# A four-layer graph network on one core: PSUM bank offsets from a table instead of register arithmetic on TensorE

## The chip, the core and the metric

The kernel runs on one core of one Trainium2 chip. The metric is the device time of one execution in microseconds (us); lower is better. Three executions of the kernel before took 2623.59, 2626.45 and 2630.86 us; the median is 2626.45 us.

## What is computed

There are 3125 nodes with 512 features and 53,125 edges (50,000 drawn, and a loop at each node), sorted by target node. Four layers follow one another; each normalizes the features, takes the positive part, applies its own graph operation and adds the result to x:

```
h = relu(layernorm(x));  x = x + relu(segment_sum((h @ W)[src] * w, dst))                     # layer 0
h = relu(layernorm(x));  x = x + relu(segment_sum(norm * (h @ W.T + b)[src], dst))            # layer 1
h = relu(layernorm(x));  x = x + mlp(h + segment_sum(h[src], dst))                            # layer 2
h = relu(layernorm(x));  x = x + gat(h, src, dst)     # layer 3: 8 heads, softmax over a node's edges
```

In every layer the heavy part is the same: for each edge a row of 512 numbers is fetched by its source node and summed into the row of its target node.

## The kernel before

Nodes are cut into 25 tiles of 125. The edges are cut into chunks of 128; since a chunk can touch two tiles, 440 **steps** cover all of them, and which tile a step belongs to depends on the data. In each layer all 440 steps run in order. Step i of a layer does this:

- **GpSimd (POOL)** issues one indirect DMA (L1758 in layers 0 to 2, L1813 in layer 3) that gathers the 128 source rows of the step, 128x512, from a table in HBM into one of 11 ring buffers. From the twelfth on it first waits on `stepped`, until the step eleven before is done with that buffer. In layer 3, 25 of the 440 gathers were made earlier (L1805).
- **VectorE (DVE)** makes `sel`, a 128x125 matrix that says which edge goes to which node (L776 in layer 0; L483 for four steps at a time in layers 1 to 3). In layer 3 it also scales the gathered rows (L1218).
- **TensorE (PE)** multiplies `sel` with the gathered rows into a PSUM bank and adds to what is there (L1456; L1452 and L1453 on two float16 halves in layer 2; in layer 3 a small second product of 8 columns, L1458). One f32 matmul of the program stands in the profile as two records.
- **ScalarE (ACT)** waits for the last step of a tile, takes the bank out (`keep_tiles`, L1266 to L1272), and sets the bank up for the tile three further on (`set_bank`), which counts up the semaphore `fresh`.

Three banks (`NAGG`) are used in turn. TensorE must know a step's bank and that it has been set up. Both depend on the step's tile number t, which is known only at run time. So TensorE's instruction queue loads the tile numbers of 20 steps into registers (`load_tiles`, L1427, every 20 steps), and for each step copies one (L1430), adds 25 for each earlier layer plus one (L1448), waits on `fresh` for that sum, and computes the sum modulo 3 and from it the address. This queue is the part of TensorE that reads instructions, waits on semaphores and works on registers (PEldq in the profile); the array behind it multiplies.

Between the steps TensorE does other work of the layer: projections of the next layer's rows (L1416), transposes (L1405), small products (L1495, L1597, L1615, L1626). Between layers 2 and 3 stands a stretch of attention scores, in which TensorE uses the tile numbers too (`target_steps`); the change leaves it as it is.

The tables of step numbers are made at the end of the start-up, beside the projection of layer 0's rows. `step_tables` is a generator on VectorE whose pieces run in the order of the code between the pieces of the projection: `rows_low` (L470), which makes the low half of a tile's rows `hTl` for the projection on TensorE (L1416). The last piece of `step_tables` starts at L608, takes the turned tables out of PSUM (L608 to L611), works out the ends of tiles (L612 to L620) and a mask (L623 to L628). After it stand the last two `rows_low`. Then TensorE projects the last two tiles, ScalarE copies them out, SyncE stores them to `table[0]`, and the first gather of layer 0 waits for that store.

## Time and profile before

| | |
|---|---|
| device time, median of three | 2626.45 us |
| span of the profiled execution, first to last instruction | 3086.3 us |
| mean granted TensorE clock in it, share of full | 0.896 |
| TensorE busy (array) | 2384.8 us, 77% |
| GpSimd busy | 1795.9 us, 58% |
| VectorE busy | 1593.7 us, 52% |
| ScalarE busy | 335.0 us, 11% |
| moved by DMA | 557.12 MB, mean 181 GB/s |

The profiled execution took 460 us longer than the median of the executions without a profile, so its durations can't be taken over one for one. Of one execution the page gives the span from the first to the last instruction and nothing around it.

A group of instructions has a line of the code, an engine, the tile that is written and those that are read, a count, the busy time and the mean of one. "idle before" is the time that the engine stood still just before, and "<-" names what ended it; "issue" means that nothing in the profile explains it. For a gather on POOL the time shown is that of issuing it, not of moving its data.

### The profile page before, as it was taken

The page shows a single profiled execution, that of the slowest core. Times are in us where ns is not written, and L with a number is a line of the kernel's source. Part 1 is how long each engine was busy: PE and PEld are TensorE (multiplying, and loading weights), DVE is VectorE, ACT ScalarE, POOL GpSimd, SP SyncE. Part 2 cuts the span into 40 slices and gives each one's busy share as a digit, 9 for nine tenths or more (in the row PEclk, how much of TensorE's full clock was granted, in tenths as well). Part 3 has the DMA queues.
Part 4 walks back from the last instruction along what each step waited for, and adds up shares of the span by engine and source line. Part 5 has one row for each costly group of instructions (what it writes and reads, how often), then busy time and mean ns, then how long its engine had stood idle before and what let it go on. Part 6 is the DMA issues. An engine that isn't in the chain of part 4 may idle for free.

```text
span 3086.3 us, 32808 instructions
## 1 busy us (share of the span) xinstructions
PE 2384.8 (77%) x8542; PEld 1265.4 (41%) x8542; DVE 1593.7 (52%) x3774; ACT 335.0 (11%) x523; POOL 1795.9 (58%) x1878
## 2 busy tenths in 40 slices
PE   7888889887678777785788888885068589988887
PEld 5534444343223222221354454453058445544444
DVE  7665555554234353332244444444059677766665
ACT  4200000000000000000000000001057310000000
POOL 0466666665466666665666666653710456666665
PEclk9898999998789888997899999997579789999999
DMA  6586666676567766666666666663134457776665
GB/s 157 174 243 180 174 180 177 187 241 177 154 192 212 203 201 205 196 193 181 184 200 198 204 200 199 204 181 80 10 101 153 136 157 211 208 222 192 194 190 171
DMA packets 212761, 557.12 MB, mean 181 GB/s; under 512 B 55433, under 2 KB 56834, under 8 KB 212601
## 3 DMA queue, kind: packets, MB, share of 16 engines
q0 software_dynamic: 144448, 462.60, 52.3%
q1 hardware_dynamic: 66970, 90.10, 9.7%
q10 hardware_dynamic: 1182, 2.33, 0.3%
q8 instruction: 96, 1.57, 0.2%
q14 instruction: 65, 0.52, 0.1%
HBM read 515.28 MB, written 39.59 MB: 180 GB/s over the span
## 4 chain that ended last, share of the span: by engine, by line
PE 51%; DVE 15%; another core or an unknown queue 13%; issue 12%; DMA 6%; POOL 2%; ACT 1%; SPq 0%; ACTq 0%; DVEq 0%; POOLq 0%
PE tiles L1456 28%; DMA ring<-table,src_t 5%; PE upper L1416 5%; PE last_bank L1597 2%; PE tiles L1453 2%; PE tiles L1452 2%; DVE sel L776 2%; PE upper L1458 2%; PE last_bank L1416 2%; PE upper L1687 1%; POOL ring L1758 1%; PE upper L1626 1%; PE upper L1405 1%; DVE stage L713 1%
## 5 line engine op out<-in xcount | busy, mean ns | idle before, releaser
L1758 POOL DMA_INDIRECT ring<-table,src_t x1320 | 1266.9, 960 | 717.8 <-issue 324.3
L1456 PE MATMUL tiles<-ring,sel 128*125 128x512 f32 x2590 | 1390.4, 652 | 264.2 <-issue 178.4
L1456 PEld LDWEIGHTS tiles<-ring,sel 128*125 128x125 f32 x2590 | 444.3, 198 | 754.6 <-issue 745.5
L1813 POOL DMA_INDIRECT ring<-table,src_t x415 | 399.0, 961 | 240.5 <-PE upper L1458 105.5
L483 DVE TENSOR_TENSOR sel<-iota_bank,dl_t 128x500 f32<-128x500 f32 (+1 forms) x330 | 221.5, 674 | 513.3 <-PE tiles L1456 226.6
L1218 DVE TENSOR_TENSOR ring<-ring,last_bank 128x512 f32<-128x512 f32 x388 | 260.5, 685 | 169.6 <-DMA ring<-table,src_t 140.6
L1458 PEld LDWEIGHTS upper<-big,sel 128*125 128x125 f32 x880 | 169.7, 193 | 222.5 <-issue 222.0
L1452 PE MATMUL tiles<-ring,sel 128*125 128x512 f16 x440 | 176.5, 401 | 61.8 <-issue 32.1
L1453 PE MATMUL tiles<-ring,sel 128*125 128x512 f16 x440 | 172.9, 393 | 10.6 <-issue 10.3
L1416 PE MATMUL upper<-wh,hTh 128*125 128x512 f32 x200 | 100.4, 502 | 73.1 <-DVE hTl L759 23.7
L1791 POOL DMA_INDIRECT big<-score_table,src_t x104 | 98.4, 946 | 81.5 <-DVE acc L988 50.1
L776 DVE TENSOR_SCALAR sel<-node_iota,dl_t,w_t 128x125 f32<-128x125 f32 x440 | 134.2, 358 | 0.3 <-PE tiles L1456 0.2
L1458 PE MATMUL upper<-big,sel 128*125 128x8 f32 x880 | 126.2, 215 | 0.6 <-issue 0.6
L713 DVE TENSOR_TENSOR stage<-iota_bank,stage 128x500 bf16<-128x500 f32 x110 | 74.3, 676 | 86.5 <-remote 60.4
L1805 POOL DMA_INDIRECT x<-table,src_t x25 | 26.3, 1052 | 155.5 <-DMA acc<-src_digits 144.6
L1452 PEld LDWEIGHTS tiles<-ring,sel 128*125 128x125 f16 x440 | 61.2, 139 | 130.0 <-issue 111.8
L1597 PE MATMUL last_bank<-big,stage 128*125 128x512 f32 x200 | 96.8, 629 | 8.9 <-issue 7.3
L1093 DVE TENSOR_REDUCE big<-upper 128x16 f32<-128x448 f32 x84 | 50.6, 618 | 83.7 <-remote 72.4
L1405 PE MATMUL upper<-ident,stage 125*128 125x125 f32 x400 | 61.6, 277 | 41.2 <-ACT stage L1231 20.6
L1416 PE MATMUL upper<-wl,hTh 128*125 128x512 f32 x200 | 93.3, 466 | 0.0
L1416 PE MATMUL upper<-wh,hTl 128*125 128x512 f32 x200 | 92.1, 461 | 0.0
L1416 PEld LDWEIGHTS upper<-wh,hTh 128*125 128x125 f32 x200 | 45.9, 230 | 98.2 <-issue 85.0
(335 smaller groups left out, 2522.2 us busy)
## 6 DMA issues: line engine op xcount, KB each, us to landing
ring<-table,src_t POOLq DMA_INDIRECT x1735
table<-stage SPq DMA_DIRECT2D x50, 224.0 KB
table<-acc SPq DMA_DIRECT2D x50, 224.0 KB
acc<-dst_places SPq DMA_DIRECT2D x28, 256.0 KB
x<-dst_places SPq DMA_DIRECT2D x27, 256.0 KB
x<-in_x SPq DMA_DIRECT2D x25, 224.0 KB
kept_x<-x SPq DMA_DIRECT2D x25, 224.0 KB
x<-kept_x SPq DMA_DIRECT2D x25, 224.0 KB
```

Source lines behind the costliest of these rows:

```text
L483: V.tensor_tensor(to, iota_p[:, None, :].to_broadcast([CE, SB, TN]), dl_t[:, i:i + SB, None].to_broadcast([CE, SB, TN]), ALU.is_equal).the ...
L713: V.tensor_tensor(lo_hot[:, i % (2 * SB):i % (2 * SB) + SB, 0:TN], iota_p[:, None, :].to_broadcast([CE, SB, TN]), s_lo[:, i:i + SB, None]. ...
L776: V.tensor_scalar(out=sel[:, i % SELS, :], in0=node_iota[:, :], scalar1=dl_t[:, i:i + 1], scalar2=w_t[:, i:i + 1], op0=ALU.is_equal, op1=A ...
L1218: V.tensor_tensor(slot, slot, weights[:, :, None].to_broadcast([CE, H, DP]), ALU.mult).then_inc(scaled, 1)
L1416: last = P.matmul(to, a[:, q, k, :], b[:, k, :], start=(k == 0 and n == 0), stop=(k == KB - 1 and n == 2))
L1452: P.matmul(to, sel16[:, n % SELS, :], ring16[:, r, 0:D], start=False, stop=True, skip_group_check=True)
L1453: last = P.matmul(to, sel16[:, n % SELS, :], ring16[:, r, D:2 * D], start=False, stop=True, skip_group_check=True)
L1456: last = P.matmul(to, sel[:, n % SELS, :], rows, start=False, stop=True, skip_group_check=True)
L1458: last = P.matmul(upper[0:TN, bass.ds(b, 1), DEN_AT:DEN_AT + H].rearrange("p a h -> p (a h)"), sel[:, n % SELS, :], exps[:, i, :], start=F ...
L1597: last = P.matmul(bank[7][0:TN, :], yT[:, b, :], raw_w[:, b, :], start=(b == 0), stop=(b == KB - 1))
L1758: G.indirect_dma_start(out=(ring16 if layer == 2 else ring)[:, n % RING, :], out_offset=None, in_=table[layer][:, :], in_offset=bass.Indir ...
L1813: G.indirect_dma_start(out=rows_at(i), out_offset=None, in_=table[3][:, :], in_offset=bass.IndirectOffsetOnAxis(ap=src_t[:, i:i + 1], axis ...
```

## The change

The step's bank and the number to wait for are put into a table, `step_row`, once, at the end of the start-up. It has 22 groups, one for each 20 steps; a group holds 20 bank offsets (t modulo 3, times 512) and 10 numbers t + 1, one for each pair of steps, taken from the pair's second step. VectorE makes it with five more instructions after L611 of before, in the last piece of `step_tables`; the count of `tables` goes from 6 to 8.

TensorE loads 30 registers every 20 steps in place of 20. It takes the bank's offset straight from a register, and it waits on `fresh` only at even steps, for the bank of the later step of the pair. `fresh` becomes four semaphores, one for each layer, so that no layer's base has to be added. The banks of each layer now begin at bank 0. Some small tiles of the start-up are laid into buffers that are free then.

```diff
             def step(layer, i):
                 n = STEPS * layer + i
                 r = n % RING
                 if i % LOADED_TILES == 0:
-                    load_tiles(i)
-                t = step_tile(i)
+                    load_banks(i)
...
-                g = t + (TILES * layer + 1)
-                P.wait_ge(fresh, g)
-                b = (g + (NAGG - 1)) % NAGG
-                to = tiles[0:TN, bass.ds(b, 1), :].rearrange("p a d -> p (a d)")
+                if i % 2 == 0:
+                    P.wait_ge(fresh[layer], loaded[LOADED_TILES + i % LOADED_TILES // 2])
+                to = flat_tiles[0:TN, bass.ds(loaded[i % LOADED_TILES], D)]
...
+            def load_banks(i):
+
+                _, loaded[:] = nc.values_load_multi_w_load_instructions(
+                    step_row[0:1, i // LOADED_TILES, :], engines=(mybir.EngineType.PE,), min_val=0, max_val=(NAGG - 1) * D,
...
                 V.tensor_copy(tile_row[:, :], bank[3][0:1, 0:STEPS]).then_inc(tables, 1)
+                tiles_of = bank[3][0:1, 0:STEPS].rearrange("p (a r) -> p a r", r=LOADED_TILES)
+                own.mark(V.tensor_scalar(out=step_banks, in0=tiles_of, scalar1=171.0, scalar2=None, op0=ALU.mult))
+                V.tensor_scalar(out=pair_tiles, in0=tiles_of[:, :, 1::2], scalar1=1.0, scalar2=None, op0=ALU.add).then_inc(tables, 1)
+                V.wait_ge(v_own, own.n)
+                own.mark(V.tensor_scalar(out=step_banks, in0=step_banks, scalar1=9, scalar2=None, op0=ALU.logical_shift_right))
+                V.wait_ge(v_own, own.n)
+                own.mark(V.scalar_tensor_tensor(out=step_banks, in0=step_banks, scalar=-float(NAGG), in1=tiles_of,
+                                                op0=ALU.mult, op1=ALU.add))
+                V.wait_ge(v_own, own.n)
+                V.tensor_scalar(out=step_banks, in0=step_banks, scalar1=float(D), scalar2=None, op0=ALU.mult).then_inc(tables, 1)
...
-                    n = (t + layer) % NAGG
+                    n = t % NAGG
```

On TensorE, the first two steps of layer 0 before; `ISA` is the register instruction that makes the address, and instructions that only copy a register or only wait are not among these rows:

```order
L1427 TENSOR_LOAD tile_row
L1448 REGISTER_ALU [waits sel_ok,got0]
L1456 ISA [waits fresh]
L1456 MATMUL tiles<-ring,sel 125x512
L1448 REGISTER_ALU [waits sel_ok,got1]
L1456 ISA [waits fresh]
L1456 MATMUL tiles<-ring,sel 125x512
```

and the first two steps of the kernel changed:

```order
L1446 TENSOR_LOAD step_row
L1476 ISA [waits fresh0,sel_ok,got0]
L1476 MATMUL tiles<-ring,sel 125x512
L1476 ISA [waits sel_ok,got1]
L1476 MATMUL tiles<-ring,sel 125x512
```

The addition is gone from every step, and with it the copy that fed it. The wait on `fresh` stands at every second step; the address instruction and the matmul stay.

On VectorE, the last piece of `step_tables` from the table of tile numbers on, before (`past`, `alone_end` and `end_row` are the ends of tiles, `masked` is the mask):

```order
L611 CAST tile_row<-iota_bank 1x440
L612 TENSOR_SCALAR past<-acc 1x25
L614 TENSOR_SCALAR alone_end<-acc 1x25
L616 TENSOR_SCALAR past<-past 1x25 [waits v_own]
L619 ISA end_row<-alone_end,past 1x50 [waits v_own]
L620 TENSOR_SCALAR tid_row<-tid 1x25
L623 TENSOR_SCALAR masked<-big 110x512 [waits tables]
```

and in the kernel changed (`acc` is where `past` and `alone_end` lie now):

```order
L613 CAST tile_row<-iota_bank 1x440
L615 TENSOR_SCALAR step_row<-iota_bank 1x22x20
L616 TENSOR_SCALAR step_row<-iota_bank 1x22x10
L618 TENSOR_SCALAR step_row<-step_row 1x22x20 [waits v_own]
L620 SCALAR_TENSOR_TENSOR step_row<-step_row,iota_bank 1x22x20 [waits v_own]
L623 TENSOR_SCALAR step_row<-step_row 1x22x20 [waits v_own]
L624 TENSOR_SCALAR acc<-acc 1x25
L626 TENSOR_SCALAR acc<-acc 1x25
L628 TENSOR_SCALAR acc<-acc 1x25 [waits v_own]
L631 ISA end_row<-acc 1x50 [waits v_own]
L632 TENSOR_SCALAR tid_row<-tid 1x25
L635 TENSOR_SCALAR masked<-big 110x512 [waits tables]
```

Five instructions on one partition, on 440 and 220 numbers, have come in ahead of the ends of tiles; three of them wait for the one before.

## Rows read from the trace of the kernel before

**Rows 1.** The page, section 1: engine, busy time (share), instructions, of each engine.

```profile
PE 2384.8 (77%) x8542; PEld 1265.4 (41%) x8542; DVE 1593.7 (52%) x3774; ACT 335.0 (11%) x523; POOL 1795.9 (58%) x1878
```

**Rows 2.** The four layers: length, busy us (count) of PE, PEld, DVE, ACT, POOL.

```profile
118.00:780.00 662.00, 550.75 (x1722) 271.42 (x1722) 379.49 (x1071) 32.53 (x55) 428.09 (x440) 0.92 0.68 196
793.00:1426.00 633.00, 484.12 (x904) 163.48 (x904) 238.75 (x593) 30.34 (x48) 422.24 (x440) 0.89 0.69 199
1436.00:2082.00 646.00, 520.65 (x1973) 298.80 (x1974) 266.72 (x625) 27.90 (x47) 416.38 (x440) 0.91 0.68 198
2485.00:3086.00 601.00, 512.53 (x1759) 279.92 (x1757) 400.46 (x803) 35.93 (x94) 387.39 (x404) 0.97 0.68 198
```

**Rows 3.** POOL by time: start us, us, instruction, [idle before <- what ended it].

```profile
1000.09 0.95 POOL L1758 DMA_INDIRECT ring<-table,src_t  x1 [0.30 <-issue]
1001.34 0.94 POOL L1758 DMA_INDIRECT ring<-table,src_t  x1 [0.30 <-issue]
...
1005.12 0.94 POOL L1758 DMA_INDIRECT ring<-table,src_t  x1 [1.17 <-remote]
```

**Rows 4.** Stretch of layer 1, POOL's gathers of L1758: length, busy us (count).

```profile
793.00:1400.00 607.00, 409.07 (x427) 0.89 0.69 201
```

**Rows 5.** The same stretch, L1456: matmuls (count), weight loads (count).

```profile
793.00:1400.00 607.00, 461.14 (x844) 154.20 (x845) 0.89 0.69 201
```

**Rows 6.** POOL in layer 0: a gather that waited for TensorE.

```profile
310.71 0.99 POOL L1758 DMA_INDIRECT ring<-table,src_t  x1 [4.29 <-PE tiles L1456]
```

**Rows 7.** Waits of TensorE: line <- who ended them: us in total, times, longest.

```profile
PE tiles L1456 <- issue: 182.3, 209, 4.5
...
PE tiles L1452 <- issue: 32.1, 43, 3.7
```

**Rows 8.** Queue instructions by line: count, ns min/median/max, first and last start.

```profile
L1430 PEldq MOVE  x4: 29/29/38, 123.9 to 125.3; - x4
...
L1448 PEldq ALU_OP  x1760: 2/32/1060, 124.1 to 3078.6; - x196
...
L1456 PEldq FUSED_REGOPS  x1320: 2/90/1388, 124.2 to 3078.7; - x189
...
L1427 PEldq TENSOR_LOAD <-tile_row x110: 13/1361/2895, 122.3 to 3049.1; - x110
...
L1261 ACTq TENSOR_LOAD <-end_row x16: 544/548/745, 125.6 to 3058.3; - x16
```

**Rows 9.** Weight loads in layer 0, matmuls in layer 3, by time.

```profile
420.33 0.19 PEld L1456 LDWEIGHTS tiles<-ring,sel 128*125 128x125 f32 x1 [0.24 <-issue]
420.76 0.19 PEld L1456 LDWEIGHTS tiles<-ring,sel 128*125 128x125 f32 x1 [0.24 <-issue]
...
2562.34 1.10 PE L1456 MATMUL tiles<-ring,sel 128*125 128x512 f32 x2
...
2563.41 1.10 PE L1456 MATMUL tiles<-ring,sel 128*125 128x512 f32 x2
```

**Rows 10.** The chain that ended last, end of start-up: start us, us, what.

```profile
103.11 0.51 DVE tile_row L611
103.62 0.09 DVE past L612
...
104.32 0.44 DVE masked L623
...
104.78 0.70 DVE masked L625
...
105.85 0.68 DVE hTl L470
...
106.67 4.30 PE last_bank L1416 x12
```

**Rows 11.** TensorE and POOL there, in order of time.

```profile
106.67 0.46 PE L1416 MATMUL last_bank<-wh,hTh 128*125 128x512 f32 x1 [2.04 <-DVE hTl L470]
...
117.78 0.96 POOL L1758 DMA_INDIRECT ring<-table,src_t  x1 [29.70 <-DMA table<-stage]
```

More of the change, by code:

```diff
@@ L139, in build @@
         tile_row = sb("tile_row", [1, STEPS], I32)
+        step_row = sb("step_row", [1, STEPS // LOADED_TILES, LOADED_TILES * 3 // 2], I32)
         end_row = sb("end_row", [1, -(-TILES // LOADED) * LOADED], I32)
-        past = sb("past", [1, TILES], I32)
-        alone_end = sb("alone_end", [1, TILES], I32)
         tid_row = sb("tid_row", [1, -(-TILES // LOADED) * LOADED], I32)
-        thr_i = sb("thr_i", [128, TILES - 1], I32)
         tid = sb("tid", [128, TILES])
@@ L187, in build @@
         flat_sel = sel[:, :, :].rearrange("p a b -> p (a b)")
+        thr_i, tile_i = (acc[:, 7, n * 32:n * 32 + TILES - 1].bitcast(I32) for n in range(2))
+        tile_f, thr = (acc[:, 7, n * 32:n * 32 + TILES - 1] for n in range(2, 4))
+        cnt = acc[0:EP, 7, 128:128 + TILES - 1]
+        past, alone_end = (acc[0:1, 6, n * 32:n * 32 + TILES].bitcast(I32) for n in range(2))
+        step_banks = step_row[:, :, 0:LOADED_TILES]
+        pair_tiles = step_row[:, :, LOADED_TILES:]
+        iota_i = stage[:, 0:TN].bitcast(I32)
         def hbuf(n):
             return stage[0:TN, n % 2 * D:(n % 2 + 1) * D]
+        zero = stage[0:RS, D:D + CE]
         def zbuf(n):
@@ L355, in build @@
         opened = signal("opened")
-        fresh = signal("fresh")
+        fresh = [signal(f"fresh{n}") for n in range(4)]
         kept = signal("kept")
@@ L621, in step_tables @@
                                 op0=ALU.mult).then_inc(tables, 1)
-                V.wait_ge(tables, 6)
+                V.wait_ge(tables, 8)
                 own.mark(V.tensor_scalar(out=masked[:, :, :], in0=rsf[:, :, 1, :], scalar1=0.0, scalar2=None, op0=ALU.is_ge))
@@ L1246, in set_bank @@
                 if layer in (1, 2):
-                    A.copy(bank[n][0:TN, :], acc[0:TN, t, :]).then_inc(fresh, 1)
+                    A.copy(bank[n][0:TN, :], acc[0:TN, t, :]).then_inc(fresh[layer], 1)
                 else:
@@ L1251, in set_bank @@
                         A.wait_ge(a_own, own.n)
-                    A.activation(bank[n][0:TN, :], ident[0:TN, 0:1].to_broadcast([TN, D]), ACT.Copy, scale=0.0).then_inc(fresh, 1)
+                    A.activation(bank[n][0:TN, :], ident[0:TN, 0:1].to_broadcast([TN, D]), ACT.Copy, scale=0.0).then_inc(fresh[layer], 1)
             end_regs = [A.alloc_register(f"end{n}") for n in range(LOADED)]
@@ L1321, in scalar_program @@
                 A.wait_ge(scaled1, t + 1)
-                set_bank((t + 1) % NAGG, 1, t)
+                set_bank(t % NAGG, 1, t)
             A.wait_ge(scaled1, TILES)
@@ L1329, in scalar_program @@
                 A.wait_ge(ln_h, 2 * TILES + t + 1)
-                set_bank((t + 2) % NAGG, 2, t)
+                set_bank(t % NAGG, 2, t)
             A.wait_ge(ln_h, 3 * TILES)
@@ L1394, in scalar_program @@
             for t in range(NAGG):
-                set_bank((t + 3) % NAGG, 3, t)
+                set_bank(t % NAGG, 3, t)
             exponentials(2)
@@ L1423, in tensor_program @@
             tile_regs = [P.alloc_register(f"tile{n}") for n in range(LOADED_TILES)]
+            loaded = []
+            flat_tiles = tiles[:, :, :].rearrange("p a d -> p (a d)")
+            flat_upper = upper[:, :, :].rearrange("p a d -> p (a d)")
             def load_tiles(i):
                 P.reg_load(tile_regs, tile_row[0:1, bass.ds(i, LOADED_TILES)])
+            def load_banks(i):
+                _, loaded[:] = nc.values_load_multi_w_load_instructions(
+                    step_row[0:1, i // LOADED_TILES, :], engines=(mybir.EngineType.PE,), min_val=0, max_val=(NAGG - 1) * D,
+                    skip_runtime_bounds_check_because="a tile's number modulo NAGG, times D, or a tile's number and one")
             def step_tile(r):
@@ L1457, in step @@
                 if layer == 3:
-                    last = P.matmul(upper[0:TN, bass.ds(b, 1), DEN_AT:DEN_AT + H].rearrange("p a h -> p (a h)"), sel[:, n % SELS, :],
+                    last = P.matmul(flat_upper[0:TN, bass.ds(loaded[i % LOADED_TILES] + DEN_AT, H)], sel[:, n % SELS, :],
                                     exps[:, i, :], start=False, stop=True, skip_group_check=True)
@@ L1502, in open_banks @@
                     P.matmul(bank[n][0:TN, :], zeros, wide, start=True, stop=True).then_inc(opened, 1)
-            P.wait_ge(tables, 6)
+            P.wait_ge(tables, 8)
             open_banks()
@@ L1775, in gpsimd_program @@
                     in_offset=bass.IndirectOffsetOnAxis(ap=gstep[:, b:b + 1], axis=0)).then_inc(rows_in, 16)
-            G.wait_ge(tables, 6)
+            G.wait_ge(tables, 8)
             G.wait_ge(rows_turned, 1)
@@ L1875, in sync_program @@
                 S.dma_start(src_digits[a].rearrange("(b p) e -> p b e", p=RS), src_rows[a]).then_inc(src_pl_out, 16)
-            S.wait_ge(tables, 6)
+            S.wait_ge(tables, 8)
             S.wait_ge(ln_h, TILES)
```

6 lines of the change are left out of this document (removed).

## The prediction

> **What bounds the kernel now.** I read the shares of busy time first, then the four layers' stretches, then what is late inside a stretch. TensorE is busy for 77% of the span [rows 1] and looks like the bound. The stretches say it less plainly: layers 0 to 3 took 662, 633, 646 and 601 us, with TensorE busy for 551, 484, 521 and 513 us of them and POOL for 428, 422, 416 and 387 us [rows 2]. Nobody is full. POOL's busy time hides a part of its beat: two gathers in a row start 1.25 us apart, 0.95 us of issuing and 0.30 us in which nothing is waited for [rows 3]. So 440 gathers take at least 440 x 1.25 = 550 us, in each of layers 0 to 2, of some 640. The rest are longer gaps, as the 1.17 us before the gather at 1005.12 [rows 3].
>
> Are these gaps waits for TensorE? A gather waits for the step eleven before it. From 793 to 1400 us POOL issued 427 gathers [rows 4], and TensorE began 844 half-steps, that is 422 steps [rows 5]. It lies 5 steps behind, not 11, so in layer 1 the ring is not what holds POOL. Counted out step by step in the trace, the wait on TensorE is what ends a gap in layer 0 at eight gathers, the longest idle time being 4.29 us [rows 6], some 17 us in all, and in layer 1 at two. So **in the profiled execution the gathers set the pace**, and TensorE runs a few microseconds behind them. The chain of waits gives TensorE half of the span, but it goes by whose semaphore came last before a gather, and that was a step that the gather had no need of.
>
> **TensorE's queue against its array.** Per step the queue runs a copy (29 ns), perhaps a wait, the addition (32 ns), and the address (90 ns) [rows 8]; these numbers leave the gaps out. Undisturbed, four copies of four steps in a row start from 123.9 to 125.3 us, so a step is 1.4 / 3 = 0.47 us of queue, about 0.1 us an instruction [rows 8]. The array needs 0.43 us for each half of an f32 step, 0.86 us a step, and 1.07 us in layer 3 with the small product [rows 9]. In layer 2 a step is two f16 halves, by half as short; there queue and array are about level, but the other work of that layer fills the array. **The queue is therefore faster than the array, runs ahead of it, and what is taken from it is hidden under the matmuls**, except where the array stands empty and the next step comes through the queue.
>
> **The change, part by part.** The additions (1760 [rows 8]) and as many copies go; the waits on `fresh` rode on the address instruction, which stays. That is two instructions a step, 0.2 us of queue, 350 us over four layers, all beside matmuls but for restarts. Restarts: TensorE began a step after idling 209 + 43 = 252 times with nothing named [rows 7]; with the named ones I say 300. There, what lay between the arriving rows and the matmul was the addition and the address; now the wait sits on the address itself, 0.1 us earlier: 30 us on TensorE if all counted. They don't, since most of these pauses are waits for gathered rows and TensorE is then caught up; only those matter where POOL waits for TensorE or a layer ends. Bounds 0 and -30; I take -1, nearest to rows 4 to 6: ten such waits and four ends of layers at 0.1 us each.
>
> The load of registers grows from 20 to 30. 20 take 1.36 us on TensorE and 8 take about 0.55 us on ScalarE, of which the trace has 16 [rows 8], so one more costs (1.36 - 0.55) / 12 = 0.07 us and the load grows by 0.7 us. 88 loads (22 in each layer) make 60 us of queue. Bounds 0 (the array has work queued) and +60; I take +1, for the same reason as above.
>
> That trade has a rule against it. The Trainium skill, on the page Runtime: NRT & Kernel Launch, section Instruction fetch mechanics, puts a register load at about 200 ns a register even in bulk. By that ten more would be 2 us a load and 176 us in 88 loads; the trace doesn't agree, since at that price the 20 of now would take 4 us where the rows have 1.36.
>
> The wait on `fresh` for the pair's later step is taken a step early at a tile's first step. Who stands behind it on TensorE's queue is one step of the tile before. But the bank was set up when the tile three before had been taken out, a tile and more (some 17 steps, over 20 us) earlier. Cost 0. Banks that begin at 0 in each layer, and four semaphores in place of one: every layer's first banks are set up after the last tile of the layer before anyway. Cost 0.
>
> The table costs where nothing hides it. VectorE's last piece of the tables is on the chain that ended last: the table of tile numbers at 103.11, the mask to 105.5, then the low half `hTl` at 105.85, then TensorE's projection at 106.67 [rows 10], for which TensorE had idled 2.04 us, and through the copy and the store the first gather at 117.78 [rows 11]. Each instruction put in ahead moves all of that. Prices: 440 numbers out of PSUM on one partition take 0.51 us, 25 numbers 0.09 us, so 220 about 0.3 us; from SBUF 512 numbers a partition take 0.44 us, and with two inputs 0.70 us [rows 10], so about 0.4 and 0.6 us for 440. The sum is 0.51 + 0.30 + 0.40 + 0.60 + 0.40 = 2.2 us, and three waits for the one before at 0.1 us: **+2.5 us**, bounds 1.9 and 3.1, all on the path.
>
> Sum: -1 + 1 + 2.5 = +2.5 us on the profiled 3086.3. The executions without a profile are 460 us shorter, and what is shorter in them no row tells. I take the difference over as it is, and round down since restarts and loads are as likely to give a little: 2626.45 + 2 = **2628 us**.
>
> **Rivals.** *The queue counts after all.* Without the profile something is faster by 15%. If it is the gathers (at a beat of 1.1 us they would need 484 us a layer, below TensorE's 551 and 521 busy in layers 0 and 2 [rows 2]), TensorE becomes the bound and each restart counts. For it: the 252 pauses without a named cause [rows 7]; against it: a full array has few restarts. With half of the 30 us and a part of the shorter queue after short products, -17 + 2.5: about 2612 us, by a range of 2600 to 2618. *The longer load counts.* The same case, other side: TensorE sets the pace, the load finds the array with less than 2 us of queued work, and the steps after it run at the array's 0.86 or 1.07 us, so that the shorter queue gives nothing back. It decides as soon as the lead of the queue is under 2.0 us at a load and over 1.4 before; at half of the 88 loads that is +30, with the table 2626 + 30 + 2.5 = 2659, at a quarter 2644. For it: the unnamed pauses can as well be loads; against it: the queue has 0.4 us to spare at each step to rebuild its lead. With the 200 ns a register of the Trainium skill (the page and section above), half of the loads would cost 88 us: 2717 us. *The change does not do what it says*, the copies moved elsewhere: then only loads and table are left, 2630, inside the forecast.
>
> **How the numbers follow.** The forecast, gathers or a full array in front and the start 2.5 us later: 0.58, from 2621 to 2634. The queue counts: 0.27. The longer load counts: 0.14. The price of the Trainium skill: 0.01. A measurement of this kernel can tell about 0.3%, 8 us, from no change. So faster 0.27, same 0.57, slower 0.16. To leave no more than 0.2 out, the range goes into both rivals: 2608 to 2642.
>
> **What would show it.** Right: in the profile after, no copies and no additions in the steps' queue, the address still 1760 times, loads of about 2.0 us; VectorE's new five from 103.6 on taking 2.2 to 2.7 us; the first gather at about 120.3; POOL's beat still 1.25 us; layers of the same length within their spread, with TensorE some 5 steps behind. Wrong: layers shorter by 4 us or more each with POOL's beat unchanged would say that the steps held POOL; shorter layers with a shorter beat would be no work of this change. More idle time of TensorE right behind each load would speak for the longer load.

## The result: 3.0% slower, and the profile after

The changed kernel takes 2707.16 us (median of four, 2704.77 to 2709.78) against 2628.05 (2623.59 to 2630.86) of the kernel before: ratio 1.0304, 95% interval 1.0289 to 1.0319. The forecast was 2628 us in a range up to 2642, so it is wrong by 79 us. Chips differ: on two of the four whose number is on record all versions that keep their gathers, before and after, take 3080 us and more instead of some 2630 (that it is the chip, and not its state at that hour, is not shown; one chip was measured at two times and was fast both times). The profile of the kernel before shown above (span 3086.3) is by its length and its gathers of that kind; its distance of 460 us from the median was not the profile's doing, since the execution profiled in experiment 1 took 3124.28 us and the others of the same kernel beside it 3114 to 3128. A later profile of the same kernel on a chip of the fast kind (the last kernel of experiment 4) has a span of 2624.7, and it is the one to compare with. The first lines of both pages, after:

```profile
span 2705.8 us, 29623 instructions
PE 2259.9 (84%) x8542; PEld 1250.3 (46%) x8542; DVE 1598.1 (59%) x3779; ACT 335.2 (12%) x523; POOL 1809.7 (67%) x1878
...
PE 66%; DVE 11%; DMA 10%; issue 9%; POOL 3%; ACT 1%; SPq 0%; ACTq 0%; DVEq 0%; POOLq 0%
```

and before, on a fast chip (the last line of each is section 4, the shares of the chain that ended last):

```profile
span 2624.7 us, 32808 instructions
PE 2273.5 (87%) x8542; PEld 1198.7 (46%) x8542; DVE 1596.8 (61%) x3774; ACT 335.0 (13%) x523; POOL 1810.8 (69%) x1878
...
PE 54%; DMA 20%; POOL 9%; DVE 8%; issue 7%; ACT 2%; SPq 0%; ACTq 0%; DVEq 0%; POOLq 0%
```

No engine is busy for longer in a way that would explain it (TensorE's array 2259.9 us, before 2273.5); the span is 81 us longer, and the chain has moved from gathers (DMA and POOL 29%, after 13%) to TensorE (54%, after 66%). By stretches, each from a layer's first gather to its last step (columns as in [rows 2]), after:

```profile
120.00:711.00 591.00, 521.91 (x1722) 262.44 (x1722) 377.36 (x1057) 31.51 (x54) 430.75 (x440) 0.94 0.75 220
729.00:1295.00 566.00, 445.75 (x904) 166.82 (x904) 238.38 (x592) 29.59 (x47) 422.89 (x440) 0.91 0.76 223
1306.00:1885.00 579.00, 495.70 (x1966) 301.09 (x1966) 269.52 (x623) 27.32 (x46) 418.66 (x440) 0.92 0.75 221
2111.00:2700.00 589.00, 515.10 (x1820) 283.61 (x1820) 427.50 (x833) 57.20 (x137) 398.33 (x415) 0.91 0.70 207
```

and before, on a fast chip:

```profile
118.00:690.00 572.00, 527.81 (x1722) 250.43 (x1722) 378.95 (x1057) 30.68 (x52) 432.00 (x440) 0.98 0.78 227
708.00:1270.00 562.00, 463.14 (x904) 146.33 (x904) 240.84 (x592) 29.59 (x47) 423.02 (x440) 0.97 0.76 224
1281.00:1842.00 561.00, 497.02 (x1972) 287.07 (x1972) 269.36 (x623) 27.89 (x47) 418.90 (x440) 0.95 0.77 228
2069.00:2619.00 550.00, 503.62 (x1820) 278.12 (x1820) 424.00 (x832) 56.89 (x137) 398.34 (x415) 0.96 0.75 221
```

The layers are longer by 19, 4, 18 and 39 us, 80 in all; the start gives 2 more, and the stretch between layers 2 and 3, which the change leaves alone, nothing. In each layer the granted clock (the number before the last two) is lower by 0.03 to 0.06.

Where inside a layer? The waits of TensorE (line <- who ended them: us in total, times, longest), after:

```profile
PE tiles L1476 <- issue: 129.7, 26, 12.1
PE tiles L1472 <- issue: 55.8, 10, 8.2
PE tiles L1476 <- DMA ring<-table,src_t: 49.8, 70, 10.7
PE tiles L1476 <- DVE ring L1230: 40.2, 9, 6.6
```

and before, on a fast chip:

```profile
PE tiles L1456 <- DMA ring<-table,src_t: 103.7, 161, 10.6
...
PE tiles L1456 <- DVE ring L1218: 28.1, 29, 2.0
...
PE tiles L1456 <- issue: 16.0, 48, 2.3
```

Before, TensorE pauses often and briefly for rows (161 times, 0.64 us each). After, it stands 26 + 10 times with nothing named, 5 us each, and 9 times behind VectorE, 4.5 us each: 45 long stops, about as many as there are second groups of 20 steps in four layers (44). The registers' loads, by line (count, ns min/median/max, first and last start; the two lines of the code that load), after:

```profile
L1442 PEldq TENSOR_LOAD <-tile_row x22: 1356/1361/1374, 1923.9 to 2086.8; - x22
L1446 PEldq TENSOR_LOAD <-step_row x88: 2356/5281/16373, 125.5 to 2667.6; - x88
```

and four loads of L1446 in a row, each in a window of its own:

```profile
L1446 PEldq TENSOR_LOAD <-step_row x1: 2396/2396/2396, 183.0 to 183.0; - x1
L1446 PEldq TENSOR_LOAD <-step_row x1: 7109/7109/7109, 205.6 to 205.6; - x1
L1446 PEldq TENSOR_LOAD <-step_row x1: 2362/2362/2362, 231.1 to 231.1; - x1
L1446 PEldq TENSOR_LOAD <-step_row x1: 7101/7101/7101, 257.1 to 257.1; - x1
```

A load of 30 registers takes 2.36 us or **7.1 us, in strict turns**. A group is 30 numbers of 4 bytes, 120 bytes; if `step_row` itself begins at a multiple of 16 bytes, every second group begins 8 bytes off one, and the first load of each layer, a short one, fits that. Groups of `tile_row` are 80 bytes, so that all of them lie alike, in this kernel and in the one before; experiment 1 moves them.

What a long load does, on TensorE by time (start us, us, instruction, [idle before <- what ended it]), around the load of 257.1 to 264.2:

```profile
256.42 1.02 PE L1476 MATMUL tiles<-ring,sel 128*125 128x512 f32 x2
...
257.94 1.02 PE L1476 MATMUL tiles<-ring,sel 128*125 128x512 f32 x2
264.42 2.07 PE L1476 MATMUL tiles<-ring,sel 128*125 128x512 f32 x2 [5.45 <-issue]
...
266.67 2.05 PE L1476 MATMUL tiles<-ring,sel 128*125 128x512 f32 x2
```

and the stretches around it (columns as in [rows 2]):

```profile
244.00:257.00 13.00, 13.00 (x48) 6.21 (x48) 9.68 (x30) 1.20 (x2) 9.70 (x11) 1.00 0.73 213
257.00:264.40 7.40, 1.97 (x12) 0.86 (x9) 3.93 (x10) 0.00 (x0) 5.57 (x7) 0.88 0.70 205
264.40:268.00 3.60, 3.58 (x9) 1.92 (x9) 0.97 (x2) 0.00 (x0) 2.78 (x3) 0.50 0.72 209
268.00:272.00 4.00, 4.00 (x14) 2.73 (x13) 0.00 (x0) 1.20 (x2) 0.94 (x1) 0.82 0.60 173
272.00:276.00 4.00, 4.00 (x17) 1.98 (x16) 2.53 (x7) 0.00 (x0) 1.22 (x2) 1.00 0.00 0
```

Three costs follow one another. The array works off what the queue had handed over, 1.9 us, and then stands for 5.45. Within that pause, at 262.6, the granted clock falls to 0.50, the level of 1.2 GHz, and it stays there until 269.4 (the rows above cut this stretch in two); a pair of matmuls takes 2.07 us instead of 1.02. Such a fall stands at 40 of the 44 long loads (between the load's start and 6 us past its end), and in a stretch as long at 5 of the 44 short ones. Then TensorE has fallen so far behind that POOL must wait for a free buffer:

```profile
268.99 0.94 POOL L1778 DMA_INDIRECT ring<-table,src_t  x1 [1.21 <-PE tiles L1476]
274.48 0.94 POOL L1778 DMA_INDIRECT ring<-table,src_t  x1 [4.54 <-PE tiles L1476]
```

POOL's waits for that line, after and then before on a fast chip (the 0.3 us that every gather has are in them, so the longest is what tells):

```profile
POOL ring L1778 <- PE tiles L1476: 115.0, 312, 4.5
```

```profile
POOL ring L1758 <- PE tiles L1456: 89.6, 294, 0.3
```

Counted gather by gather in the two traces: before, POOL never idles for more than 0.6 us between two gathers of a layer in layers 0 to 2; after, it does 25 times, and in 22 of them the step that it needed had ended less than 0.3 us before. Beyond the usual 0.3 us these gaps add up to 15.5, 3.5 and 16.0 us in layers 0, 1 and 2, which is most of the 19, 4 and 18 us lost. In layer 3 it is 24 such gaps and 53 us, where there was one of 18. So (argued from these sums, not tested alone) a stop of the array costs time as far as it makes the gathers wait.

### The profile page after: what moved, and what is told of

Same layout as the page of the kernel before. It is cut to its first block, busy times and chain, and to the rows that moved or that the text cites. A ratio compares the mean times of both kernels' runs of the same rounds, so it can differ in the third digit from the quotient of the medians.

```text
span 2705.8 us, 29623 instructions
## 1 busy us (share of the span) xinstructions
PE 2259.9 (84%) x8542; PEld 1250.3 (46%) x8542; DVE 1598.1 (59%) x3779; ACT 335.2 (12%) x523; POOL 1809.7 (67%) x1878
## 4 chain that ended last, share of the span: by engine, by line
PE 66%; DVE 11%; DMA 10%; issue 9%; POOL 3%; ACT 1%; SPq 0%; ACTq 0%; DVEq 0%; POOLq 0%
PE tiles L1476 37%; DMA ring<-table,src_t 9%; PE upper L1428 5%; PE tiles L1472 3%; PE tiles L1473 3%; PE last_bank L1617 3%; PE upper L1646 3%; PE last_bank L1428 3%; POOL ring L1778 2%; PE upper L1417 2%; PE upper L1478 2%; PE upper L1707 1%; POOL ring L1833 1%; PE upper L1515 1%; DVE sel L485 1%
## 5 line engine op out<-in xcount | busy, mean ns | idle before, releaser
L1476 PE MATMUL tiles<-ring,sel 128*125 128x512 f32 x2590 | 1351.6, 645 | 243.2 <-issue 129.7
L1476 PEld LDWEIGHTS tiles<-ring,sel 128*125 128x125 f32 x2590 | 453.2, 198 | 674.7 <-issue 670.2
L1472 PE MATMUL tiles<-ring,sel 128*125 128x512 f16 x440 | 182.5, 415 | 94.5 <-issue 55.8
L1473 PE MATMUL tiles<-ring,sel 128*125 128x512 f16 x440 | 179.3, 407 | 0.0
L1811 POOL DMA_INDIRECT big<-score_table,src_t x104 | 106.6, 1025 | 82.5 <-DVE acc L1000 51.1
L1472 PEld LDWEIGHTS tiles<-ring,sel 128*125 128x125 f16 x440 | 64.0, 145 | 151.9 <-issue 132.0
L1428 PE MATMUL upper<-wh,hTh 128*125 128x512 f32 x200 | 89.9, 450 | 3.6 <-DVE hTl L472 1.8
L1280 ACT ACTIVATE acc<-tiles,dis 125x512 f32<-125x512 f32 x25 | 17.2, 687 | 552.0 <-PE tiles L1476 552.0
L1282 ACT ACTIVATE acc<-tiles 125x512 f32<-125x512 f32 x25 | 14.9, 598 | 559.9 <-PE tiles L1473 559.9
L1278 ACT ACTIVATE acc<-tiles 125x512 f32<-125x512 f32 x25 | 14.9, 598 | 552.5 <-PE tiles L1476 552.5
L1473 PEld LDWEIGHTS tiles<-ring,sel 128*125 128x125 f16 x440 | 65.1, 148 | 38.4 <-issue 18.2
L1428 PE MATMUL upper<-wl,hTh 128*125 128x512 f32 x200 | 80.5, 402 | 0.0
```

What stands on the lines that cost most here:

```text
L1428: last = P.matmul(to, a[:, q, k, :], b[:, k, :], start=(k == 0 and n == 0), stop=(k == KB - 1 and n == 2))
L1472: P.matmul(to, sel16[:, n % SELS, :], ring16[:, r, 0:D], start=False, stop=True, skip_group_check=True)
L1473: last = P.matmul(to, sel16[:, n % SELS, :], ring16[:, r, D:2 * D], start=False, stop=True, skip_group_check=True)
L1476: last = P.matmul(to, sel[:, n % SELS, :], rows, start=False, stop=True, skip_group_check=True)
```

## The experiments

The theory from here on is called **place**: a load whose first byte is not on a multiple of 16 bytes costs TensorE's queue three times as much, and time is lost where neither the queue's lead over the array nor TensorE's slack towards the gathers covers it. The rivals: the number of registers by itself; the rest of the change.

### 1. The place of the loads, either way (on a chip where the kernel before takes 3114 us)

Groups of 32 places, 128 bytes, each on a multiple of 16. Small tiles are moved for the room.

```diff
-        step_row = sb("step_row", [1, STEPS // LOADED_TILES, LOADED_TILES * 3 // 2], I32)
+        step_row = sb("step_row", [1, STEPS // LOADED_TILES, 32], I32)
```

> The kernel changed, with one edit: each group of 30 numbers in step_row has 32 places, so that every group begins at a multiple of 16 bytes in memory (120 bytes apart before, so every second group began 8 bytes off). Some small tiles of the start-up move to make room. Theory 'place': the loads of TensorE's queue took 2.36 us and 7.1 us in turn because of that offset; now all 88 take 2.36 us, and the time falls from 2707 to about 2632 (2626 + 2.5 for the table + some for 1 us more per load). Rival 'number': it is the 30 registers, or that matmuls read the loaded registers themselves; the long ones stay, 2707. Rival 'banks and waits': the new order of banks or the wait for a pair costs the time; loads shorten but the time stays above 2690.

Measured: 3103.84 us, ratio 0.9956 (0.9936 to 0.9976). The times expected here and in the next two texts were meant for a chip with the kernel before at some 2626 us; on this one the length of the loads is what tells. The median of the 88 loads is 2.36 us, in odd groups as in even ones.

Groups of 31 places, 124 bytes, which begin 0, 12, 8 and 4 bytes off in turn:

```diff
+        step_row = sb("step_row", [1, STEPS // LOADED_TILES, 31], I32)
```

> The kernel changed, with groups of 31 places: they begin 0, 12, 8 and 4 bytes off a multiple of 16 in turn. Theory 'place', if only a multiple of 16 is fast: a load of 2.36 us, then three of about 7.1 us, in turn. If 8 bytes were enough it would have been fast before, so 8 is slow in any case; whether 4 and 12 are slower than 8 is open. Time: 66 slow loads in place of 44, so 2707 + 40 = 2745. Rival 'number': the pattern of two stays, or all alike.

Measured: 3130.97 us, one execution, 0.5% above the 3114.45 of the kernel before. The loads' row:

```profile
L1443 PEldq TENSOR_LOAD <-step_row x88: 2362/7085/11580, 125.9 to 3091.3; - x88
```

The first nine take 2.57, 7.11, 7.08, 7.09, 2.37, 7.15, 7.09, 7.08 and 2.36 us: one in four is short, the one on a multiple of 16. So 4, 8 and 12 bytes off cost the same.

The kernel before, unchanged, as a measure:

> The kernel before, unchanged, for a profile of an execution that is as long as the executions without a profile; the first one was 460 us longer. Expected: a span near 2626 us; register loads on TensorE's queue still 1.36 us each, all 110 alike; gathers on POOL 1.25 us apart with few longer gaps. If TensorE set the pace (the rival 'the queue counts'), POOL's gaps over 1.25 us would end with a step of TensorE; if the gathers do, they end with nothing of TensorE.

Measured: 3119.41 us, ratio 1.0015 (0.9993 to 1.0038). The 2626 us expected did not come: this chip takes some 3115 us with a profile or without.

The kernel before with nothing of the change, only its table 8 bytes further on:

```diff
-        tile_row = sb("tile_row", [1, STEPS], I32)
+        tile_row = sb("tile_row", [1, STEPS + 4], I32)[:, 2:STEPS + 2]
```

> The kernel before, with one edit: the row of tile numbers begins 8 bytes further on, so that all 110 loads of 20 registers begin 8 bytes off a multiple of 16. Theory 'place': a load takes about 0.2 us a register, 4 to 5 us in place of 1.36, and the kernel becomes slower by 60 to 150 us (88 loads in the layers with 3.3 us more each make 290 us of queue; in the kernel changed 44 loads with 5.7 us more and 44 with 1 us more, also 295 us, cost 80 us; here they are spread over twice as many loads). Rivals 'number' and 'banks and waits': 1.36 us each and 2626.

Measured: 3207.84 us, ratio 1.029 (1.0241 to 1.0339). The row stands where [rows 8] had 1361 ns:

```profile
L1427 PEldq TENSOR_LOAD <-tile_row x110: 1932/4742/7371, 122.1 to 3172.8; - x110
```

**The place alone, with 20 registers and the old steps, makes a load 3.5 times as long.** Off the multiple of 16 it is 4.74 / 20 = 0.237 us a register and 7.1 / 30 = 0.237: a price by the register. On it, 1.36 and 2.36.

### 2. The changed kernel itself on the slower kind of chip (kernel before: 3089 us)

Unchanged, then with groups of 32 places; then with a wait for a bank once in five steps, so that a group has 24 places, 96 bytes; then the kernel before with loads of 30 registers, the last ten unused.

```diff
-        step_row = sb("step_row", [1, STEPS // LOADED_TILES, LOADED_TILES * 3 // 2], I32)
+        step_row = sb("step_row", [1, STEPS // LOADED_TILES, LOADED_TILES * 6 // 5], I32)
...
-                if i % 2 == 0:
-                    P.wait_ge(fresh[layer], loaded[LOADED_TILES + i % LOADED_TILES // 2])
+                if i % 5 == 0:
+                    P.wait_ge(fresh[layer], loaded[LOADED_TILES + i % LOADED_TILES // 5])
```

> The changed kernel unchanged, on the same chip as the three beside it. The theory 'place' says that every second group of its table begins 8 bytes off a multiple of 16 and that those 44 loads take 7.1 us of TensorE's queue instead of 2.4. How much of it shows depends on which chip it is. Where the kernel before takes some 2628 us, TensorE is close behind the gathers, and the 3.0% of the first measurement come back: 2707 us, plus or minus 5. On a chip as the one of the first four runs, where the kernel before takes 3114 us, the gathers come slower and TensorE has time to catch up behind a load: at most +0.8%, with groups of 31 places as the upper bound (3131, one run). The rival 'the kind of chip makes no difference' says +3.0% on either: 3208 on the slower chip.

> The changed kernel with its groups padded from 30 to 32 places, so that each of the 88 loads begins on a multiple of 16 bytes; all else is as in the changed kernel. 'Place' says all loads at 2.36 us and nothing left of the slowdown: on a chip with the kernel before at 2628 us between 2600 and 2650 us, and on one with 3114 again some 3104 (ratio 0.994 to 0.998). The rival 'the thirty registers themselves cost' says that 1.0 us more in 88 loads is still exposed to a good part, 2628 + 2.5 + 88 x 0.5 = 2675 us (ratio 1.01 and more).

> The changed kernel with TensorE waiting for a bank once in five steps instead of once in two, so that a group is 20 offsets and 4 banks, 24 places of 4 bytes, 96 bytes, every group on a multiple of 16. By 'place' a load takes 1.36 + 4 x 0.10 = 1.8 us and the time is at or a little below the one with groups of 32 places, by 0 to 88 x 0.6 = 53 us less. The rival 'thirty registers make a load slow' would give the same for this kernel, and is told apart by the one with groups of 32 alone. If the steps' waits cost anything by themselves, 264 fewer of them show as a shorter time than the load explains.

> The kernel before, whose 88 loads for the steps of the layers fetch 30 registers instead of 20, the last ten unused; the loads stay on multiples of 16 bytes (steps of 80 bytes), and nothing else changes. It measures by itself what 1.0 us more of queue in each load costs: 2.36 us against 1.36. 'The array has queued work behind which it hides' gives 0 to +8 us (ratio 1.000 to 1.003); 'the load is bare' gives up to +88 us (1.033 where the kernel before takes 2628). If the load were to cost more here than in the changed kernel with groups of 32, the shorter queue of that kernel is what makes up for it.

Measured, in this order: 3096.36 (ratio 1.0017, 0.9998 to 1.0036), 3081.18 (0.9972, 0.9951 to 0.9993), 3081.24 (0.9971, 0.9954 to 0.9989) and 3089.12 us (1.0005, 0.9987 to 1.0022). The first two are the same kernel with and without the long loads, side by side. The long loads are there as before (the same 7.1 us), and they cost 15 us, the distance of the first two, where the fast chip loses 79. The rival "the kind of chip makes no difference" is out. Counted load by load in the trace (time without a matmul between a load's start and the first matmul after its end), the array stands 226 us beside long loads here and 236 us in the first profile after: the stops are the same, and what differs is whether anyone misses the time. POOL's gathers on this chip, whose gaps of 1.9 us or 1.2 us stand between rows at the old beat of 1.25:

```profile
1013.93 0.95 POOL L1778 DMA_INDIRECT ring<-table,src_t  x1 [0.30 <-issue]
1016.79 0.94 POOL L1778 DMA_INDIRECT ring<-table,src_t  x1 [1.91 <-PE tiles L1476]
```

Such gaps are rare in the fast chip's trace of layer 1: there the gathers start 1.27 us apart on average, and here 1.42. Where they come from is not settled; TensorE, which the row names, had finished the step needed at least 0.45 us before in 56 of the 63 gaps of layer 1 that are longer than 0.35 us.

### 3. Gathers left out, so that TensorE is short of time (kernel before: 2625 us)

Every eighth gather is not made, in the kernel before, the changed one, and the one with groups of 32 places. The expectations were written for a chip of the slower kind; these three ran on one of the fast kind, where TensorE is shorter of time still.

```diff
+                    if left_out(n):
+                        continue
...
-            return 16 * (n // RING + 1)
+            return 16 * sum(not left_out(m) for m in range(n % RING, n + 1, RING))
+        def left_out(n):
+            return n % 8 == 7 and n % STEPS >= RING
```

> The kernel before with every eighth gather of the four layers left out: POOL skips it, and TensorE works on the rows that the buffer still holds, so that the output isn't the reference's. TensorE's steps, loads, waits and banks stay as they are. It is meant to bring a chip on which a layer's gathers start 1.42 to 1.48 us apart on average to the 1.27 to 1.32 us of the first profile of the changed kernel (1.42 x 7 / 8 = 1.24). Expected where the kernel before takes 3090 to 3115 us: shorter by 3 x 440 / 8 = 165 places at some 1.45 us, less what TensorE then sets itself, so 2870 to 3000 us. If the time doesn't fall by at least 60 us the gathers did not set the pace there either, and the theory that slower gathers hide the long loads falls.

> The changed kernel with the same eighth of the gathers left out (its output isn't the reference's). Theory 'the long loads cost as much as TensorE is short of time': with the gathers out of the way 44 loads of 7.1 us are bare by some 1 to 2 us each and more in the last layer, so that it is 40 to 100 us longer than the kernel before with the same gathers left out (1.4 to 3.4%), where on such a chip without leaving any out it was 8 us (0.2%). The rival 'the chips differ in something else, and the loads cost 8 us here whatever the gathers do' gives a difference of under 15 us.

> The changed kernel with groups of 32 places and the same eighth of the gathers left out (its output isn't the reference's). 'Only the place of the load': within 10 us of the kernel before with the same gathers left out, or below it by up to 30 us if the shorter queue now counts; and 40 to 100 us below the changed kernel with these gathers left out. Rival 'thirty registers and the place both count': 20 to 40 us above the kernel before.

Measured: 2402.93, 2603.68 and 2412.10 us. The kernel before falls by 222 us (ratio 0.9155, 0.9136 to 0.9175), so on the fast kind, too, the gathers set its pace. With fewer gathers the changed kernel is 201 us (8.4%) behind the kernel before, and with groups of 32 places 9 us (0.4%). **44 loads, each 4.74 us longer than its neighbours, are 208 us of queue; groups of 32 places take 192 us away, so nearly the whole of it shows once little else is waited for.** Of the other 9 us the start has some 2.5; whether the rest is the 1 us more in each load is not shown. I had expected 40 to 100, with the queue's lead as a cushion at each load. The cushion is there, but the lower clock behind each stop takes back nearly as much. The same span of both, with the long and then with the short loads (columns as in [rows 2]):

```profile
118.00:2600.00 2482.00, 2143.33 (x8123) 1182.81 (x8121) 1506.86 (x3509) 279.49 (x415) 1601.31 (x1652) 0.92 0.67 196
```

```profile
118.00:2402.00 2284.00, 2085.15 (x8121) 1142.89 (x8120) 1502.26 (x3507) 279.32 (x415) 1603.48 (x1652) 0.96 0.73 212
```

Of 198 us, 58 are the same matmuls at a lower clock (0.92 against 0.96), and 140 are standing still (339 against 199). That it is the clock is borne out by the sum: busy time weighted by the clock granted in it is 2013 us with the long loads and 2028 with the short ones. So of the 208 us of queue the lead covers some 68, and the clock adds 58.

### 4. Nothing left out, on a fast chip (kernel before: 2626 us)

> The changed kernel with groups of 32 places, all loads on multiples of 16 bytes. On a chip with the kernel before at 2625 us, 'the place is all of it' says 2610 to 2635 us (ratio 0.994 to 1.004): the 79 us are gone, the start costs 2.5 us and the shorter queue may give some back. 'The thirty registers have a part' says 2640 us and more. Where the kernel before takes some 3100 us it is 0.996 or 0.997 again, and tells nothing new.

> The changed kernel with a wait for a bank once in five steps and groups of 24 places, loads of 1.6 us where groups of 32 places have 2.36. If 0.74 us of queue in each of 88 loads is bare on a chip with the kernel before at 2625 us, it is up to 65 us below the kernel with groups of 32 places; if it is behind queued work, both are level within 8 us, as they were to 0.1 us on the slower kind of chip.

> The kernel before with 30 registers a load in place of 20, the last ten unused: 1.0 us more of queue in each of 88 loads, on multiples of 16 bytes. 'Behind queued work': 0 to +8 us on a chip with the kernel before at 2625 us (ratio 1.000 to 1.003). 'Bare': up to +88 us (1.033).

> The kernel before, unchanged, for a profile on the chip of the three beside it: ratio 1.000 within 0.3%. On a chip where it takes 2625 us: gathers at a beat of 1.25 us and layers 0 to 2 of 560 to 600 us, with few of the gaps of 2 us in POOL that the first profile had; the stretch between layers 2 and 3 some 140 us shorter than there.

Measured: 2628.16 (ratio 1.0006, 0.9996 to 1.0016), 2627.84 (1.0011, 1.0002 to 1.0020), 2628.17 (1.0008, 0.9999 to 1.0018) and 2625.03 us (0.9999, 0.9989 to 1.0009). **Two numbers of padding in each group take the 79 us back**, and the time is that of the forecast. (The two ratios, 1.0304 and 1.0006, were not measured on one chip at one time; side by side the two stand in experiments 2 and 3.) Thirty registers on a multiple of 16 cost nothing that can be told (third kernel), and a wait once in five steps is level with one in two (second). The loads with groups of 32 places:

```profile
L1443 PEldq TENSOR_LOAD <-step_row x88: 2356/2367/10541, 126.6 to 2597.1; - x88
```

### 5. The table off the start-up chain, and the old loads off their place (kernel before: 2626 us)

VectorE's five instructions are put behind the last `hTl`, with a semaphore of their own for which TensorE waits ahead of a load; 24 registers as above. Then the kernel before with its table 8 bytes on, as in experiment 1.

```diff
-                tiles_of = bank[3][0:1, 0:STEPS].rearrange("p (a r) -> p a r", r=LOADED_TILES)
...
             for _ in beside:
                 pass
+            tiles_of = tile_row[:, :].rearrange("p (a r) -> p a r", r=LOADED_TILES)
...
             def load_banks(i):
+                P.wait_ge(banks_ok, 2)
```

> The kernel with 24 registers a load, with VectorE's five instructions of the table taken out of the start-up chain: they read the table of tile numbers in SBUF instead of PSUM and stand behind the low half hTl, where VectorE idles for 8 us. If the 2.5 us on that chain are all that the aligned kernels lose, the first gather starts at 118.2 instead of 120.8 and the time is 2 to 3 us below the version with the table on the chain: within 1 us of the kernel before (ratio 0.999 to 1.001) where that takes 2625 us. The rival 'the shorter queue or the rarer waits give something, and the start hid it' says 2618 us and less (0.997).

> The kernel before with its table of tile numbers 8 bytes further on, so that all 110 loads of 20 registers take 4.7 us instead of 1.36; nothing else is changed. TensorE's queue runs up to 4.3 us ahead of the array where the array is full and 0.9 where it waits for rows, so such a load leaves the array idle for 0.4 to 3.9 us. On a chip with the kernel before at 2625 us: 22 x 3.4 = 74 us in the stretch between layers 2 and 3, where the array waits for each load, and 0 to 22 x 1 us in each layer, 2700 to 2790 us (ratio 1.03 to 1.06). On one with 3100, 1.029 again. A ratio under 1.01 would say that only the loads of the changed kernel are dear.

Measured: 2622.95 us, ratio 0.9984 (0.9974 to 0.9993), and 2752.03 us, ratio 1.047 (1.0449 to 1.0490). The first is 3 us below the kernel before, where within 1 us was expected. By the ratios it is some 7 us (give or take 3) below the same kernel with the table on the chain, the second of experiment 4, of which the start is 2.0 (its first gather stands at 120.23); the two ran on different chips, and what the rest is stays open. The first gathers on POOL, after, before on a fast chip, and in this kernel:

```profile
120.37 0.97 POOL L1778 DMA_INDIRECT ring<-table,src_t  x1 [31.68 <-DMA table<-stage]
```

```profile
118.19 0.96 POOL L1758 DMA_INDIRECT ring<-table,src_t  x1 [29.68 <-DMA table<-stage]
```

```profile
118.20 0.96 POOL L1780 DMA_INDIRECT ring<-table,src_t  x1 [29.70 <-DMA table<-stage]
```

The second, old code with loads of 4.75 us, loses 126 us. From the traces of it and of experiment 4's last kernel (first to last step of each layer): 7, 4, 11 and 19 us in layers 0 to 3 and 86 in the stretch between 2 and 3. In that stretch the array stands 81 us beside the 22 loads where it stood 12, near the 22 x 3.4 = 75 us by which they are longer. In layers 0 to 3 it stands 49, 86, 68 and 45 us beside them and the layers lose a part of that only: least in layer 1, where the queue has the least lead and the array stands longest, but where TensorE has the most slack towards the gathers. So the price of a load is what neither the queue's lead nor that slack covers.

## Why the prediction was wrong

- **The gathers set the pace, TensorE behind them: right.** On the fast chip, before, POOL's beat is 1.25 us as in [rows 3], and with an eighth of the gathers left out the time falls by 222 us (experiment 3). But the cover was thin: TensorE is busy for 528 of 572, 497 of 561 and 504 of 550 us in layers 0, 2 and 3, and 463 of 562 in layer 1, the one that loses only 4 us. The 460 us between the profile and the times were taken for something of the profile; they were another chip, with more slack. The rivals saw that the slack might be less without them.
- **The shorter queue is hidden: right.** The address instruction fell from 90 to 37 ns, and copies and additions are gone. By line, after and before (count, ns min/median/max):

```profile
L1476 PEldq FUSED_REGOPS  x1320: 37/37/43, 128.2 to 2694.3; - x189
```

```profile
L1456 PEldq FUSED_REGOPS  x1320: 88/90/117, 124.5 to 2616.1; - x189
```

  With the loads in place this gives between nothing and 3 us (experiments 4 and 5), within the bounds of 0 and 30, and no gain with fewer gathers either (+9 us).
- **The load, +1 us with bounds 0 and +60: the step that failed.** Two things were wrong in it: the length of the load, and that the array's queued work would hide it. The price of 0.07 us for one more register came from two rows, 20 and 8 registers, and gave 2.06 us. The short loads take 2.36, 0.10 us for one more: a small miss. The miss that counts is that the line through two rows was laid through loads whose groups are 80 and 32 bytes, whole multiples of 16, and the change makes groups of 120 bytes. Half of the loads take 7.1 us. The term was then 44 x 5.7 + 44 x 1.0 = 295 us of queue where 60 stood, and the upper bound of the range was drawn from the same line. The queue's lead, some 4.3 us where the array is full, hides a load of 2.4 us but not one of 7.1, and 79 us of the 295 came through. The size of a group, 30 x 4 bytes, could be read in the diff; that it mattered could not be seen in any row of before.
- **The price of the Trainium skill** (page Runtime: NRT & Kernel Launch, section Instruction fetch mechanics), about 200 ns a register, was set aside because the rows had 68. It got a chance of 0.01, and its 2717 us is the nearest of all cases. That is luck: it has 2 us more on half of the 88 loads and all of that bare, where the trace has 5.7 us more on half of them and only about a third of that came through. The runs show both: 237 ns a register off the multiple of 16, 68 to 79 on it. What case the page's price was measured on no run here shows. A price that a row contradicts by a factor of three asks what its case and the row's differ in, and not only which is right.
- **The rival "the longer load counts", 0.14: its mechanism is the one that came.** It said that a load is bare when it is longer than the queue's lead. With 2.0 us it would not have been (experiment 4, loads of 2.36 us: 0 to 3 us); with 7.1 it is. So its condition came true by a length that it had not foreseen. The sign named for it, idle time of TensorE right behind each load, is what the waits show. It left out that the clock falls with such a stop.
- **The wait once in two steps, and banks from 0, at no cost: right.** Once in two and once in five are level (2628.16 and 2627.84).
- **The table, +2.5 us on the start-up chain: right.** The chain that ended last, after (start us, us, what):

```profile
104.22 0.52 DVE step_row L615
104.74 0.29 DVE step_row L616
105.03 0.31 DVE step_row L618
...
105.36 0.61 DVE step_row L620
...
106.00 0.38 DVE step_row L623
```

  From 104.22 to 106.38 it is 2.2 us, within the 2.2 to 2.7 named. The first gather starts at 120.37, where 120.3 was forecast; against the fast chip's 118.19 it is 2.2 us later. With the loads in place the kernel is 2.4 us above the kernel before (2628.16 and 2625.76).

So one term was wrong, by its assumption and not by its arithmetic; the rest of the sum stands at 2628 us once that assumption is made true.

## What to carry to other kernels

A bulk load of registers has a price that depends on where its first byte lies: lay the groups out so that each begins on a multiple of 16 bytes, even if numbers are wasted, and look at min and max of the load's row, not at its median. An unchanged length in a profile is a price for unchanged layout only; when a change alters a stride, bound the price by a row with another stride, or leave the bound open upward. What a stop on the queue costs is read from the queue's lead and from the engine's slack in that stretch, and it is worth asking whether the profile's chip has more slack than the one that is timed.

## What was not expected of the hardware

- A load of registers from SBUF on TensorE: 20 registers 1.36 us on a multiple of 16 bytes, 4.74 off it; 24 registers 1.62; 30 registers 2.36 and 7.1. Off by 4, 8 or 12 bytes is the same.
- The queue's lead over the array is small. Load by load, its length less the array's stop beside it is 4.3 us in the median of the long loads in layers 0 and 3 with fewer gathers (in layer 3 the same 4.31 at nine of eleven), 5.6 at the most in that trace, and 0.8 in the median of layer 1, where the array waits for rows. What bounds it no run here tells.
- In a stop of 5.45 us the granted clock fell to 0.50, and it was full again 5 us after the array had started anew. From 118 us on it stood at 0.50 for 431 us in the changed kernel and for 207 us in the kernel before on a fast chip.
- 12 of the 44 long loads after took 7.6 to 10.4 us, and one 16.4 (at 2350.8 us); one of the short ones of the kernel with groups of 32 took 10.5 (at 2291.4), while none of the kernel before on the fast chip took over 2.9. Many of them are the same loads in every trace: the tenth of layer 3, which took the 16.4 and the 10.5, took 13.3 and 11.5 on the slower chips and 15.5 with fewer gathers, so for this one at least it is no chance event of one execution. What held them is open, and no run here tells.
- Two kinds of chip: the kernel before takes 2625 to 2628 us on one kind and 3089 to 3114 on the other. The gathers have gaps on the latter that no engine explains, and the stretch between layers 2 and 3 takes some 400 us instead of 260.
